# Feed-forward part of a float32 transformer block: row turns by VectorE and SBUF copies in place of TensorE transposes

## What is computed

```python
x = _layernorm(x + h, ln1_g, ln1_b)            # y: made by the attention pass, stored to y_d
h2 = jax.nn.gelu(x @ w1 + b1, approximate=False) @ w2 + b2     # 512 -> 2048 -> 512
x = _layernorm(x + h2, ln2_g, ln2_b)
# and at the end of the block, per row: input + this + a gated branch (r_d)
```

## Time and profile before

| | |
|---|---|
| three runs | 3478.65, 3483.64, 3487.95 us |
| span of the profiled execution | 3482.2 us |
| TensorE busy | 3422.0 us (98%) |
| VectorE, ScalarE, GpSimd busy | 2468.2 (71%), 1969.8 (57%), 1105.2 (32%) us |
| DMA | 409.83 MB, mean 118 GB/s |

### The profile page before, as it was taken

The page is one execution under the profiler, slowest core; times in us unless marked ns, Lnnn a source line. Parts: engine busy times, 40 slices in busy tenths (PEclk is TensorE's granted clock), DMA queues, the critical chain, the costliest instruction groups (busy, mean ns, idle before and its releaser), DMA issues.

```text
span 3482.2 us, 77456 instructions
## 1 busy us (share of the span) xinstructions
PE 3422.0 (98%) x29993; PEld 3151.9 (91%) x29993; DVE 2468.2 (71%) x4839; ACT 1969.8 (57%) x4240; POOL 1105.2 (32%) x861
## 2 busy tenths in 40 slices
PE   8999999999899999999999999999999999999998
PEld 6888888888788888888888889999999999999998
DVE  6767777677667777677777766666666666666666
ACT  6777777777556666666656654444444444444443
POOL 3554554545345454555555532000000000000000
PEclk9999999999899999999999999999999999999999
DMA  3222222222323333232332346444444444444443
GB/s 128 80 77 74 95 77 83 77 74 77 107 79 114 106 102 115 82 126 94 102 109 93 111 144 206 147 148 148 147 146 146 146 146 146 146 146 146 146 147 126
DMA packets 195355, 409.83 MB, mean 118 GB/s; under 512 B 27440, under 2 KB 52528, under 8 KB 194992
## 3 DMA queue, kind: packets, MB, share of 16 engines
q1 hardware_dynamic: 194992, 404.89, 34.6%
HBM read 292.50 MB, written 112.33 MB: 116 GB/s over the span
## 4 chain that ended last, share of the span: by engine, by line
PE 70%; DVE 2%; ACT 1%; issue 0%; POOL 0%; DMA 0%; ACTq 0%; POOLq 0%; DVEq 0%
PE ffn_hidden L175 30%; PE attend_gated L175 20%; PE ffn_result L175 8%; PE attend_num L175 6%; PE attend_feat L1425 3%; PE attend_feat L1445 1%; PE ffn_turn L1910 1%; PE attend_turn L1415 1%; DVE attend_kvz_lo L1393 1%; DVE attend_pT_lo L1354 1%; PE attend_feat L1452 1%; PE attend_turn L1434 0%; ACT attend_kvz_hi L1300 0%; DVE attend_kvz_lo L1396 0%; DMA ffn_r_in<-in_L_attn_w_dram 0%
## 5 line engine op out<-in xcount | busy, mean ns | idle before, releaser
L175 PE MATMUL ffn_hidden<-ffn_yT_hi,ffn_wa_hi 128*128 128x256 f32 x2048 | 574.1, 280 | 3.5 <-DVE ffn_wa_lo L1798 1.8
L175 PE MATMUL ffn_hidden<-ffn_yT_lo,ffn_wa_hi 128*128 128x256 f32 x2048 | 573.3, 280 | 0.0
L175 PE MATMUL ffn_hidden<-ffn_yT_hi,ffn_wa_lo 128*128 128x256 f32 x2048 | 572.0, 279 | 0.0
L316 POOL TENSOR_TENSOR ffn_n_rstd<-ffn_n_base,ffn_n_power 128x2 f32<-128x2 f32 x32 | 27.5, 860 | 1300.1 <-DVE ffn_n_negmean L311 1300.1
L1780 ACT ACTIVATE ffn_ht_hi<-ffn_hs 128x512 fp32r<-128x512 f32 x248 | 156.4, 631 | 420.6 <-DVE ffn_hs L1827 420.6
L175 PEld LDWEIGHTS ffn_hidden<-ffn_yT_hi,ffn_wa_hi 128*128 128x128 f32 x2048 | 385.0, 188 | 4.4 <-DVE ffn_wa_lo L1798 2.3
L175 PEld LDWEIGHTS ffn_hidden<-ffn_yT_hi,ffn_wa_lo 128*128 128x128 f32 x2048 | 385.2, 188 | 0.0
L175 PEld LDWEIGHTS ffn_hidden<-ffn_yT_lo,ffn_wa_hi 128*128 128x128 f32 x2048 | 384.9, 188 | 0.2
L635 POOL TENSOR_TENSOR keys_z_sum<-keys_z_sum,keys_e 128x512 f32<-128x512 f32 x192 | 259.6, 1369 | 232.9 <-ACT keys_e L703 232.9
L1831 DVE TENSOR_TENSOR ffn_ht_lo<-ffn_hs,ffn_ht_hi 128x512 fp32r<-128x512 f32 x248 | 173.6, 700 | 218.9 <-ACT ffn_ht_hi L1780 218.9
L1765 ACT ACTIVATE ffn_hid<-ffn_hidden,ffn_bias 128x256 f32<-128x256 f32 x496 | 206.1, 467 | 180.5 <-PE ffn_hidden L175 180.5
(11 more groups left out here) (305 smaller groups left out, 11669.3 us busy)
## 6 DMA issues: line engine op xcount, KB each, us to landing
ffn_tq<-part_d SPq DMA_DIRECT2D x248, 512.0 KB, 3.9
keys_xin<-in_L_attn_x_dram SPq DMA_DIRECT2D x32, 512.0 KB, 4.5
xn_d<-keys_xn SPq DMA_DIRECT2D x32, 512.0 KB, 3.0
xT_d<-keys_xT_whole SPq DMA_DIRECT2D x32, 512.0 KB, 2.6
u_d<-keys_uq SPq DMA_DIRECT2D x32, 512.0 KB, 3.1
shared_xTf<-xT_d SPq DMA_DIRECT2D x32, 512.0 KB, 6.0
shared_uq<-u_d SPq DMA_DIRECT2D x32, 512.0 KB, 4.9
r_d<-shared_gate SPq DMA_DIRECT2D x32, 512.0 KB, 3.1
```

What stands on the lines that cost most here:

```text
L175: last = pe.matmul(out, stationary[a], moving[b], start=start and n == 0, stop=stop and n == len(TERMS) - 1)
```

## The change

For groups 2 to 31 the rows are no longer turned by TensorE. VectorE turns the loaded rows in blocks of 32x32 (`blocks`, two instructions of 128x512, written into `r_in`). Such a turn stays within 32 partitions each, so sixteen copies from SBUF to SBUF (`cross`, 32 partitions x 1 KB each, issued by SyncE between `t` 2 and `t` 3) bring the blocks to the right partitions, written into `y`. ScalarE and VectorE make yT.hi and yT.lo from there, in SBUF, at the same place of their lists. Since y is overwritten, the residual is loaded a second time from DRAM straight into `yb`, by SyncE between `t` 4 and `end`, and the bias is added to it just before `base` on VectorE. The load of y moves to the end of SyncE's list, two groups ahead; the loads of x_in and r_in wait until the copies have landed.

```diff
@@ -1533,6 +1533,8 @@
         s = sb("s", [P, TG, D])
         x_in = sb("x_in", [P, TG, D])
         r_in = sb("r_in", [P, TG, D])
+        y_blocks = r_in[:, :, :].rearrange("p t (h n) -> p (t h) n", h=2)
+        y_cross = y[:, :, :].rearrange("p t (h n) -> p (t h) n", h=2)
         yT = Pair(mem, ctx, "yT", [P, NC, GT])
         hid = [sb(f"hid{n}", [P, 2, GT]) for n in range(2)]
         hT = [Pair(mem, ctx, f"hT{n}", [P, 2, GT]) for n in range(HB)]
@@ -1559,6 +1561,8 @@
         w2_done, summed = sem("w2_done"), sem("summed")
         sum_ready, normed, gained, offsets = sem("sum_ready"), sem("normed"), sem("gained"), sem("offsets")
         base_ready, done, stored = sem("base_ready"), sem("done"), sem("stored")
+        blocks_made, crossed, y_hi, y_split, yb_loaded = (sem("blocks_made"), sem("crossed"), sem("y_hi"), sem("y_split"),
+                                                          sem("yb_loaded"))
 
 
 
@@ -1579,18 +1583,19 @@
         ns = len(stages)
 
         PE_BODY = [("w1", 1, 0), ("w1", 2, 0), ("w2", 0, 0), ("w1", 3, 0), ("w2", 1, 0), ("w1", 4, 0), ("w2", 2, 0),
-                   ("w1", 5, 0), ("w2", 3, 0), ("w1", 6, 0), ("w2", 4, 0), ("turn", 0, 1), ("w1", 7, 0), ("w2", 5, 0),
+                   ("w1", 5, 0), ("w2", 3, 0), ("w1", 6, 0), ("w2", 4, 0), ("w1", 7, 0), ("w2", 5, 0),
                    ("w2", 6, 0), ("w1", 0, 1), ("w2", 7, 0)]
         ACT_BODY = [("w1", 1, 0), ("hs", 1, 0), ("w1", 2, 0), ("end", 0, -1), ("hs", 2, 0), ("w1", 3, 0), ("hs", 3, 0),
                     ("w1", 4, 0), ("hs", 4, 0), ("w1", 5, 0), ("hs", 5, 0), ("w1", 6, 0), ("hs", 6, 0), ("turn", 0, 1),
                     ("w1", 7, 0), ("hs", 7, 0), ("w1", 0, 1), ("hs", 0, 1)]
-        DVE_BODY = [("w1", 1, 0), ("hs", 1, 0), ("stats", 0, -1), ("w1", 2, 0), ("hs", 2, 0), ("w1", 3, 0), ("hs", 3, 0),
-                    ("final", 0, -1), ("yb", 0, 0), ("w1", 4, 0), ("hs", 4, 0), ("w1", 5, 0), ("hs", 5, 0), ("base", 0, 0),
+        DVE_BODY = [("w1", 1, 0), ("hs", 1, 0), ("stats", 0, -1), ("blocks", 0, 1), ("w1", 2, 0), ("hs", 2, 0),
+                    ("w1", 3, 0), ("hs", 3, 0), ("final", 0, -1), ("w1", 4, 0), ("hs", 4, 0), ("w1", 5, 0), ("hs", 5, 0),
+                    ("yb", 0, 0), ("base", 0, 0),
                     ("w1", 6, 0), ("hs", 6, 0),
                     ("turn", 0, 1), ("w1", 7, 0), ("hs", 7, 0), ("w1", 0, 1), ("hs", 0, 1), ("end", 0, 0)]
         POOL_BODY = [("end", 0, 0)]
-        SP_BODY = [("t", 2, 0), ("t", 3, 0), ("t", 4, 0), ("end", 0, -1), ("base", 0, 0), ("t", 5, 0), ("t", 6, 0),
-                   ("t", 7, 0), ("t", 0, 1), ("t", 1, 1)]
+        SP_BODY = [("t", 2, 0), ("cross", 0, 1), ("t", 3, 0), ("t", 4, 0), ("yb", 0, 0), ("end", 0, -1), ("base", 0, 0),
+                   ("t", 5, 0), ("t", 6, 0), ("t", 7, 0), ("t", 0, 1), ("t", 1, 1), ("y", 0, 2)]
 
         def run(eng, do, order, head=()):
             for job, n, g in head:
@@ -1600,6 +1605,14 @@
                     if g + lead < G:
                         do(job, n, g + lead)
 
+        def from_cross(m):
+
+            return y_cross.rearrange("p i (c s) -> p c i s", s=KD)[:, 4 * m:4 * m + 4]
+
+        def in_tiles(part, m):
+
+            return part[:, 2 * m:2 * m + 2, :].rearrange("p c (t i s) -> p (c t) i s", t=TG, i=NC)
+
         def step(g, n):
 
             return NH * (g - 1) + n
@@ -1620,6 +1633,22 @@
                     sp.wait_ge(left.squared, TG * G)
                     sp.wait_ge(left.y_stored, 16)
                     sp.dma_start(y[:, :, :], y_g[0]).then_inc(y_loaded, 16)
+                elif job == "y":
+                    if g == 2:
+                        for m in range(2):
+                            sp.wait_ge(turn[m].full, 2)
+                    else:
+                        wait_alone(sp, y_split, 2 * (g - 2), sp_passed)
+                    sp.dma_start(y[:, :, :], y_g[g]).then_inc(y_loaded, 16)
+                if job == "cross":
+                    wait_alone(sp, blocks_made, g - 1, sp_passed)
+                    for i in range(NC):
+                        for j in range(NC):
+                            sp.dma_start(y_cross[j * KD:(j + 1) * KD, i, :], y_blocks[i * KD:(i + 1) * KD, j, :])\
+                                .then_inc(crossed, 16)
+                if job == "yb":
+                    sp.wait_ge(done, g)
+                    sp.dma_start(yb[:, :, :], y_g[g]).then_inc(yb_loaded, 16)
                 if job == "weights":
                     if n == 0:
                         sp.wait_ge(left.mix_full, 2 * G)
@@ -1651,14 +1680,14 @@
                     sp.dma_start(f32(tq[k % NQ][:, :, :, :]), part_d[n][:, 2:4, :, :]).then_inc(tq_loaded[k % NQ], 16)
                 if job == "base":
 
-                    for m in range(2):
-                        sp.wait_ge(turn[m].full, g + 1)
-                    wait_alone(sp, yb_ready, g + 1, sp_passed)
                     if g == 0:
+                        for m in range(2):
+                            sp.wait_ge(turn[m].full, 1)
+                        wait_alone(sp, yb_ready, 1, sp_passed)
                         sp.wait_ge(left.y_stored, 16 * G)
                         sp.wait_ge(left.r_stored, 16 * G)
-                    if g < G - 1:
-                        sp.dma_start(y[:, :, :], y_g[g + 1]).then_inc(y_loaded, 16)
+                        sp.dma_start(y[:, :, :], y_g[1]).then_inc(y_loaded, 16)
+                    wait(sp, crossed, 16 * NC * NC * min(g, G - 2))
                     wait_alone(sp, base_ready, g, sp_passed)
                     wait(sp, stored, 16 * g)
                     if g == 0:
@@ -1674,7 +1703,7 @@
                     sp.dma_start(out_g[g], x_in[:, :, :]).then_inc(stored, 16)
 
             def rest():
-                run(sp, do, SP_BODY)
+                run(sp, do, SP_BODY, (("y", 0, 2),))
                 do("end", 0, G - 1)
 
             return do, rest
@@ -1729,8 +1758,12 @@
                         for m in range(2):
                             act.wait_ge(hidden[m].full, bank_use(g, m))
                     for m in range(2):
-                        act.wait_ge(turn[m].full, g + 1)
-                        act.activation(yT.hi[:, 2 * m:2 * m + 2, :], halves(turn[m]), ACT.Copy).then_inc(yT_hi, 1)
+                        if g < 2:
+                            act.wait_ge(turn[m].full, g + 1)
+                            act.activation(yT.hi[:, 2 * m:2 * m + 2, :], halves(turn[m]), ACT.Copy).then_inc(yT_hi, 1)
+                        else:
+                            act.wait_ge(crossed, 16 * NC * NC * (g - 1))
+                            act.activation(in_tiles(yT.hi, m), from_cross(m), ACT.Copy).then_inc(y_hi, 1)
                 if job == "w1" and g == 0:
                     bank = hidden[n % HB]
                     if n == 0:
@@ -1799,6 +1832,11 @@
                             .then_inc(w_split, 1)
                 if job == "turn":
                     for m in range(2):
+                        if g >= 2:
+                            dve.wait_ge(y_hi, 2 * (g - 2) + m + 1)
+                            dve.tensor_tensor(in_tiles(yT.lo, m), from_cross(m), f32(in_tiles(yT.hi, m)), ALU.subtract)\
+                                .then_inc(y_split, 1)
+                            continue
                         dve.wait_ge(yT_hi, 2 * g + m + 1)
                         dve.tensor_tensor(yT.lo[:, 2 * m:2 * m + 2, :], halves(turn[m]),
                                           f32(yT.hi[:, 2 * m:2 * m + 2, :]), ALU.subtract).then_inc(turn[m].free, 1)
@@ -1839,10 +1877,16 @@
                     dve.wait_ge(base_ready, g + 1)
                     dve.tensor_tensor(x_in[:, :, :], x_in[:, :, :], offset[:, :].unsqueeze(1).broadcast_to([P, TG, D]),
                                       ALU.add).then_inc(offsets, 1)
+                if job == "blocks":
+                    dve.wait_ge(y_loaded, 16 * g + 16)
+                    dve.wait_ge(base_ready, g - 1)
+                    for t in range(TG):
+                        last = dve.transpose(y_blocks.rearrange("p j (c t s) -> p t c j s", c=NC, t=TG)[:, t],
+                                             y[:, t, :].rearrange("p (c j r) -> p c j r", c=NC, j=NC))
+                    last.then_inc(blocks_made, 1)
                 if job == "yb":
-                    dve.wait_ge(y_loaded, 16 * g + 16)
-                    dve.wait_ge(done, g)
-                    dve.tensor_tensor(yb[:, :, :], y[:, :, :], bias2[:, :].unsqueeze(1).broadcast_to([P, TG, D]), ALU.add)\
+                    dve.wait_ge(yb_loaded, 16 * g)
+                    dve.tensor_tensor(yb[:, :, :], yb[:, :, :], bias2[:, :].unsqueeze(1).broadcast_to([P, TG, D]), ALU.add)\
                         .then_inc(yb_ready, 1)
                 if job == "final" and g > 0:
                     dve.wait_ge(normed, TG * g + TG)
@@ -1912,9 +1956,11 @@
                         last.then_inc(turn[m].full, 1)
                 if job == "w1":
```

(4 more changed lines are left out.)

## The result

The changed kernel takes 3676.05 us (3672.37 to 3681.17) beside 3481.40 for the kernel before on the same chip: 1.0554 times as long, interval 1.0539 to 1.0569. That is 194.6 us more, 6.3 for each of the 31 intervals between loads of x. The forecast was 3505, in a range up to 3542: the direction was right, the size far outside.

A forecast was written before the change was run, and what follows sets the result against it. TensorE was taken to bound the feed-forward stage. Per pass, 0.87 us saved and 1.6 us of stall gave + 0.73, times 30 = + 22 us on the 3483.64 median: 3505 us, range 3458 to 3542.

The forecast's parts named there:

- What bounds the kernel, and what the transposes are worth: Feed-forward stage: TensorE is never idle, so dropping its eight transposes saves 0.87 us a pass, 26.1 us over 30 passes.
- The transposes on VectorE: VectorE, behind the statistics: two 128x512 float32 transposes take 1.28 us together, covered by a later 2.17 us wait for ScalarE.
- dear turn: Rival, on VectorE: the two transposes take 2.56 us, adding 2.0 us a pass, 3544 us in all; chance 0.12.
- The pitch of the copies: SyncE, between `t` 2 and `t` 3: sixteen copies issued 0.455 us apart, 7.3 us in all, delaying `t` 3 to 2842.6.
- The landing of `t` 3: DMA load behind the copies: lands 3.4 to 3.9 us after its issue, at 2846.0 to 2846.5.
- first stall: TensorE, before its first matmul using `t` 3: waits 0.4 to 1.0 us because that load lands late.
- The second stall: TensorE, at `w2` 6: late store and r delay VectorE's `base` by 2.4 us, so TensorE waits 1.6 us.
- The later wins: TensorE, each pass: both predicted stalls shift the same engine, so only the later counts, 1.6 us, not their sum.
- The upper bound of the pitch: SyncE's copy issues: at most 0.65 us each, half of the pair at L1134, 10.4 us for sixteen.
- The copies fit: Rival, on SyncE: short copies need only 0.32 to 0.38 us each, `t` 3 lands in time, say 3462 us; chance 0.25.
- Copies one by one: Rival, on SyncE: each copy waits for the previous landing, 2.7 us each, turned rows 20 us late, about 4090; chance 0.02.
- Only the first stall: Rival, on SyncE's queue: store not held back, only `t` 3 costs, 0.4 to 1.0 us, say 3480 us; chance 0.15.

## Why the prediction was wrong

**What bounds the kernel, and what the transposes are worth: right.** TensorE without a gap meant that removing its work pays; with SyncE out of the way 0.68 us a pass came, of 0.87 predicted.

**The transposes on VectorE: right.** 1.30 us for the pair against 1.28 taken, and no delay from it. The rival "dear turn" falls. So does the estimate worked out from the Trainium skill's page VectorE: DVE Perf Modes, section The three transpose paths, 2.5 us; the measurement decides, 1.30 for the pair in float32.

**The pitch of the copies: the step that failed.** I took 0.455 us from rows of loads and copies that all had DRAM on one side. A copy within SBUF takes 0.63. Sixteen times 0.175 is 2.8 us of the 3.3 by which `t` 3 went out later than I had it. The stores of rows 9 cost 0.65 each, close to what came, and I had made them the bound instead of the price. To lay the two passes over each other: VectorE's job behind the blocks starts at 2841.05, 1.30 of which are new, against 2834.04, so the pass after is shifted by 5.71; `t` 3's 2851.57 is 2845.86 there, and I had 2842.6.

**The landing of `t` 3: too small.** 4.7 us where 3.4 to 3.9 was taken. `t` 4, the residual and the store go out within 1.5 us behind it, which is the likely cause; no run isolates it. The copies' bytes are not it: with half of them TensorE waited as long for tq, 112.3 us in 2300 to 3400 against 108.8. Together the first stall became 4.8 instead of 0.4 to 1.0.

**What a stall does to the clock: not in the sum.** I counted a stall at its own length. Behind each TensorE worked for some 3 to 6 us at half the granted clock, which is the lower of its two levels, 1.2 instead of 2.4 GHz, and that cost another 2.0 us a pass, a third of the loss. The Trainium skill's page TensorE: Matmul & The Clock Gate, section Why this matters for your kernels, warns of such gaps between bursts of matmuls; the trace agrees, 0.57 from 2856 to 2860 us behind a stall of 4.8. In the kernel before there was no gap in this stage from which it could be read.

**The second stall: right in kind, and hidden.** The store landed 7.5 us after its issue where I had 5.6, and r then took 5.3 from its issue to `base` (5.4 taken). So `base` was late by 2866.25 - 5.71 - 2853.14 = 7.4 us where I had 2.4: laid over each other in the same way, the store went out 3.4 us later than I had it and took 1.9 longer to land. "The later wins" was the right rule, but TensorE had by then been held up for longer by the first stall and its clock, so that only 1.5 us of waits for VectorE's halves show in 1100. The run with `t` 5 moved brings this stall out, at 101 us.

**The range: narrower than its own bounds.** The upper bound of the pitch stood in the working, 0.65, and with it `t` 3 would go out at 2845.75 and land by 2849.2 to 2849.7: a first stall of 3.5 to 4 and, with - 0.87, some 80 to 95 us in all, 3565 to 3580. The range stopped at 3542, at the rival "dear turn", which is another cause. The bound was written down and then not used. Even with it the time would have been some 100 us short of the one measured: the landing and the clock come on top.

**The rivals.** "The copies fit" needed a pitch under 0.40. "Copies one by one" falls as well: a copy landed 1.8 us after its issue, and the next was issued 0.63 behind it. "Only the first stall" has the right place and the wrong size. What did happen, a first stall large enough to bring the clock down, stood nowhere.

## What to carry to other kernels

An engine that issues DMAs is a resource with a price for each issue: count its issues, take the price from a copy of the same kind (the same two ends and shape), and list everything queued behind them with the time at which each is wanted. When several things are late behind one queue, moving one of them forward shows the next; take the long job off the queue, or reorder all of them together. A stall of a busy TensorE costs more than its length when the granted clock falls behind it.

## What the runs showed that was not expected

- An issue of an SBUF-to-SBUF copy took 0.63 us from SyncE's and ScalarE's queue, on SyncE whether 8, 16 or 32 KB were moved; from GpSimd 0.50, also while VectorE was busy. With DRAM at one end it took SyncE 0.46 (32 KB) to 0.48 (128 KB), but 0.65 in the stores of rows 9. Why the ends matter, and what else does, is not shown here.
- Landing of a 512 KB store behind three loads of the same size: 7.6 us (median of the changed kernel), 3.0 in the kernel before, where it goes out alone.
- Behind a stall of 4.8 us the granted clock was 0.57 over the next four microseconds; in the kernel with eight copies, with 0.85 us of stalls a pass, it was 1.00 as a mean.
